# Two graph-attention layers: keys and values of all blocks first, queries and skip part behind them

## The reference

```python
# layer 0
h = layer_norm(x, g1, b1)
q, k, v = h @ Wq + bq, h @ Wk + bk, h @ Wv + bv        # 8 heads of 16
e = sum(q[dst] * k[src], -1) / 4
alpha = softmax of e over the edges of one target
att = segment_sum(alpha * v[src], dst) @ Wo + bo
x1 = x + att;  y = x1 + gelu(ln(x1) @ W1 + bf1) @ W2 + bf2
x = layernorm(x + y)
# layer 1
q, k, v = x @ Wq + bq, x @ Wk + bk, x @ Wv + bv
k_j, v_j = k[src] + edge_attr @ We, v[src] + edge_attr @ We
conv = segment_sum(alpha * v_j, dst) + x @ Wskip + bskip
h = ln(conv + x);  y = ln(gelu(h @ Wf1 + bf1) @ Wf2 + bf2 + h)
out = layernorm(x + y)
```

## Time and profile before

| | |
|---|---|
| three runs | 1785.43, 1789.74, 1793.72 us (median 1789.74) |
| span of the profiled execution | 1423.2 us, 28503 instructions |
| time outside the recorded span (median less span) | 366.5 us |
| DVE busy | 1076.5 us (76%) |
| PE busy | 1072.8 us (75%) |
| POOL busy | 901.0 us (63%), 810.3 of it the gathers |
| ACT busy | 840.3 us (59%) |
| projection, layer 0 | about 25 to 64 us |
| batches, layer 0 | 66 to 625 us |
| node stage, layer 0 | 625 to 700 us |
| projection, layer 1 | 702 to 749 us |
| batches, layer 1 | 750 to 1317 us |
| node stage, layer 1 | 1317 to 1423 us |

### The profile page before, as it was taken

The page is one execution under the profiler, slowest core; times in us unless marked ns, Lnnn a source line. Parts: engine busy times, 40 slices in busy tenths (PEclk is TensorE's granted clock), DMA queues, the critical chain, the costliest instruction groups (busy, mean ns, idle before and its releaser), DMA issues. The chain is left out here.

```text
span 1423.2 us, 28503 instructions
## 1 busy us (share of the span) xinstructions
PE 1072.8 (75%) x6809; PEld 956.7 (67%) x6809; DVE 1076.5 (76%) x2695; ACT 840.3 (59%) x2605; POOL 901.0 (63%) x1028
## 2 busy tenths in 40 slices
PE   3937678767877787768896788888888888887790
PEld 1436677667866776758735677787787778776690
DVE  5538877787877787865443888988988898897557
ACT  1615776676667666644443467766776676576351
POOL 2177777777777777531046777777777777770453
PEclk9967877787777777778897989999999999898795
DMA  5385555555555565420024567667766766671001
GB/s 157 106 182 178 173 188 194 191 155 189 193 186 159 192 193 171 137 91 0 7 79 141 176 211 223 197 193 220 214 199 196 224 207 189 219 229 48 1 1 45
DMA packets 100659, 222.50 MB, mean 156 GB/s; under 512 B 34875, under 2 KB 49882, under 8 KB 96941
## 3 DMA queue, kind: packets, MB, share of 16 engines
q0 software_dynamic: 39936, 109.11, 26.8%
q1 hardware_dynamic: 57927, 109.78, 22.8%
q10 hardware_dynamic: 2662, 2.05, 0.5%
HBM read 184.86 MB, written 36.00 MB: 155 GB/s over the span
## 5 line engine op out<-in xcount | busy, mean ns | idle before, releaser
L464 POOL DMA_INDIRECT KV<-kv_table,idx x832 | 810.3, 974 | 301.5 <-issue 247.4
L732 PE MATMUL PS<-QT,OHT 128*128 x1664 | 401.6, 330 | 146.5 <-DVE OHT L990 122.3
L732 PEld LDWEIGHTS PS<-QT,OHT 128*128 128x128 f32 x1664 | 317.9, 236 | 166.1 <-issue 164.6
L733 PE MATMUL PS<-QT,OHT 128*128 x1664 | 390.4, 324 | 0.0
L733 PEld LDWEIGHTS PS<-QT,OHT 128*128 128x128 f32 x1664 | 319.1, 238 | 0.0
L592 ACT ACTIVATE AGG<-AGG,PC,RCS x800 | 309.3, 387 | 3.1 <-ACT AGG L588 2.4
L1008 DVE TENSOR_TENSOR PR<-KV,PS 128x512 f32<-128x512 f32 x208 | 140.6, 676 | 105.6 <-DMA KV<-kv_table,idx 103.7
L778 PE MATMUL PS<-OH,KV 128*128 128x128 f32 x1600 | 208.4, 280 | 2.9 <-DVE OH L1110 1.2
L588 ACT ACTIVATE AGG<-PS 128x127 f32 x800 | 208.0, 260 | 1.0 <-issue 0.7
L778 PEld LDWEIGHTS PS<-OH,KV 128*128 128x128 f32 x1600 | 196.7, 197 | 5.6 <-issue 2.6
L584 ACT ACTIVATE PC<-PS 128x4 f32<-128x4 f32 x200 | 33.5, 168 | 267.1 <-PE PS L778 256.0
(11 more groups left out here) (158 smaller groups left out, 1352.2 us busy)
## 6 DMA issues: line engine op xcount, KB each, us to landing
REL<-rel_dram SPq DMA_DIRECT2D x52, 512.0 KB, 4.4
window_dram<-OH SPq DMA_DIRECT2D x25, 1024.0 KB
OH<-window_dram SPq DMA_DIRECT2D x50, 512.0 KB, 6.1
KV<-kv_table,idx POOLq DMA_INDIRECT x832
EA<-in_edge_batch SPq DMA_DIRECT2D x52, 256.0 KB
kv_table<-KV SPq DMA_DIRECT2D x52, 128.0 KB, 1.7
X<-in_x SPq DMA_DIRECT2D x2, 832.0 KB, 10.1
GATES<-edge_gates SPq DMA_DIRECT2D x8, 208.0 KB, 10.0
```

The costliest lines, as they stand in the source:

```text
L464: g.indirect_dma_start(KV[:, s, j, :], None, kv_table, bass.IndirectOffsetOnAxis(ap=idx[:, s, j:j + 1], axis=0)).then_inc(gathered[s][hh], 16)
L732: te.matmul(o, OHT[:, q // 2, 0, e0:e0 + P], QT[:, ds(blk, P)], start=True, stop=False)
L733: last = te.matmul(o, OHT[:, q // 2, 1, e0:e0 + P], QT[:, ds(blk + P, P)], start=False, stop=True)
```

## The change

The blocks that ACT takes out of PSUM after turning now stay on chip, all 26, in the columns of `AGG` (named `HT`), which is not in use yet at that time. PE first turns every block and multiplies it into keys and values alone (256 columns, L711 as before). After the last block it goes over all blocks again for the queries (128 columns, L718) and in layer 1 the skip part (another 128), in banks 6 and 7. These two passes are no hardware loops on PE. DVE first normalises all blocks, then takes out all queries. ACT's `keys_values` waits for PE's projection instead of DVE's queries; ACT waits once, ahead of layer 0, for the clearing of `AGG`. On POOL the adding of the bias row to `X` moves behind the gathers of layer 1 and is done for four blocks at once.

```diff
+        HT = AGG[:, 0:NP]
...
-                    pipelined(pool, (keep, 4), (shift, 0))
+                    blocks(pool, keep)
...
                 else:
+                    pool.wait_ge(*done("batch_step", NB))
+                    for b, w in quads:
+                        x3 = X[:, b * P:(b + w) * P].rearrange("p (b d) -> p b d", b=w)
+                        g.tensor_tensor(x3, x3, GB[:, 3, :].unsqueeze(1).broadcast_to([P, w, D]), ALU.add).then_inc(S["x_shifted"], w)
...
                 def turned(n, k):
                     act.wait_ge(*done("tp_ready", n + (2 * NB * l + 1)))
-                    act.wait_ge(*done("proj_ready", n + (NB * l - 1)))
+                    ht = HT[:, ds(n * P, P)]
...
                 def keys_values(n, k):
-                    act.wait_ge(*done("q_made", n + (NB * l + 1)))
+                    act.wait_ge(*done("proj_ready", n + (NB * l + 1)))
                     act.wait_ge(*done("kv_free", n + (NB * l - 3)))
-                    sc.activation(kv_out[k], PS[2 + k % 2][:, D:3 * D], ACT.Copy).then_inc(S["kv_copied"], 1)
+                    sc.activation(kv_out[k], PS[2 + k % 2][:, 0:2 * D], ACT.Copy).then_inc(S["kv_copied"], 1)
...
-                    te.matmul(PS[2 + k][:, 0:Wd], ones3[:, :], Bp[l], start=True, stop=False)
-                    te.matmul(PS[2 + k][:, 0:Wd], hT[k], Wp[l][:, :], start=False, stop=True).then_inc(S["proj_ready"], 1)
-
-                pipelined(pe, (turn, 2), (project, 0))
+                    te.matmul(PS[2 + k][:, 0:2 * D], ones3[:, :], Bp[l][:, D:3 * D], start=True, stop=False)
+                    te.matmul(PS[2 + k][:, 0:2 * D], HT[:, ds(n * P, P)], Wp[l][:, D:3 * D], start=False, stop=True).then_inc(S["proj_ready"], 1)
+
+                def project_rest(n, k):
+                    pe.wait_ge(*done("q_made", n + (NB * l - 1)))
+                    for m in range(l + 1):
+                        o, w = PS[6 + k][:, m * D:(m + 1) * D], slice(3 * m * D, (3 * m + 1) * D)
+                        te.matmul(o, ones3[:, :], Bp[l][:, w], start=True, stop=False)
+                        last = te.matmul(o, HT[:, ds(n * P, P)], Wp[l][:, w], start=False, stop=True)
+                    last.then_inc(S["rest_ready"], 1)
+
+                for n in range(-2, NB):
+                    if n + 2 < NB:
+                        turn(n + 2, n % 2)
+                    if n >= 0:
+                        project(n, n % 2)
+                for n in range(NB):
+                    project_rest(n, n % 2)
...
-                pipelined(dve, (normal, 3), (queries, 0))
+                blocks(dve, normal)
+                blocks(dve, queries)
```

More of the change, by code:

```diff
@@ L177, in build @@
             pool_go sp_go stat_step moment_step var_ready sd_ready rs_ready
-            xn_ready tp_ready ht_ready proj_ready q_made x_kept
+            xn_ready tp_ready ht_ready proj_ready rest_ready q_made x_kept
             ln_affine ln_last att_ready res_ready hidden_ready gelu_ready ffn_ready ffn_added
@@ L549, in turned @@
                     act.wait_ge(*done("tp_ready", n + (2 * NB * l + 1)))
-                    act.wait_ge(*done("proj_ready", n + (NB * l - 1)))
+                    ht = HT[:, ds(n * P, P)]
                     if l == 0:
-                        sc.activation(hT[k % 2], PS[k % 2][:, 0:P], ACT.Identity, bias=gb[:, 1:2], scale=gb[:, 0:1]).then_inc(S["ht_ready"], 1)
+                        sc.activation(ht, PS[k % 2][:, 0:P], ACT.Identity, bias=gb[:, 1:2], scale=gb[:, 0:1]).then_inc(S["ht_ready"], 1)
                     else:
-                        sc.activation(hT[k % 2], PS[k % 2][:, 0:P], ACT.Copy).then_inc(S["ht_ready"], 1)
+                        sc.activation(ht, PS[k % 2][:, 0:P], ACT.Copy).then_inc(S["ht_ready"], 1)
                 def keys_values(n, k):
-                    act.wait_ge(*done("q_made", n + (NB * l + 1)))
+                    act.wait_ge(*done("proj_ready", n + (NB * l + 1)))
                     act.wait_ge(*done("kv_free", n + (NB * l - 3)))
-                    sc.activation(kv_out[k], PS[2 + k % 2][:, D:3 * D], ACT.Copy).then_inc(S["kv_copied"], 1)
+                    sc.activation(kv_out[k], PS[2 + k % 2][:, 0:2 * D], ACT.Copy).then_inc(S["kv_copied"], 1)
+                if l == 0:
+                    act.wait_ge(*done("gates_made", 4))
                 pipelined(act, (turned, 2), (keys_values, 0), slots=4)
@@ L651, in _ @@
                 one_hots(0)
-                act.wait_ge(*done("gates_made", 4))
                 written_out(round)
@@ L699, in _ @@
             for l in range(2):
-                Wd = (3 + l) * D
                 def turn(n, k):
@@ L977, in queries @@
                     at = ds(n * P, P)
-                    dve.wait_ge(*done("proj_ready", n + (NB * l + 1)))
+                    dve.wait_ge(*done("rest_ready", n + (NB * l + 1)))
                     if l:
                         dve.wait_ge(*done("x_kept", n + 1))
-                        v.tensor_tensor(Y[:, at], PS[2 + k][:, 3 * D:4 * D], X[:, at], ALU.add).then_inc(S["batch_step"], 1)
-                    v.tensor_scalar(QT[:, at], PS[2 + k][:, 0:D], 0.25, None, ALU.mult).then_inc(S["q_made"], 1)
+                        v.tensor_tensor(Y[:, at], PS[6 + k][:, D:2 * D], X[:, at], ALU.add).then_inc(S["batch_step"], 1)
+                    v.tensor_scalar(QT[:, at], PS[6 + k][:, 0:D], 0.25, None, ALU.mult).then_inc(S["q_made"], 1)
                 def one_hots1(n):
```

## The result

| | runs | median us | ratio, 95% interval |
|---|---|---|---|
| kernel before | 1785.43 to 1793.72 | 1791.08 | |
| changed kernel | 1847.91 to 1857.87 | 1852.57 | 1.035 (1.031 to 1.039) |

A forecast was written before the change was run, and what follows sets the result against it. Layer 0 was taken as bound by POOL's gathers, layer 1 by DVE and PE handing work to each other. Terms -8.1 + 2.0 - 8.9 - 2.5 + 3.0 = -14.5 from 1789.7 gave 1775.2 us, range 1764 to 1789.

The forecast's parts named there:

- I leave that remainder alone: Whole kernel: the 366.5 us between recorded span and runs' median stay unchanged, as the change touches neither inputs nor outputs.
- Keys and values alone: PE's first pass: 0.94 us a block at full clock; first gather 8.1 us earlier in layer 0, 15.2 in layer 1.
- The straight line through two widths: PE's matmul times at 384 and 512 columns, extended to 0.53 and 0.21 us for 256, 0.31 and 0.155 for 128.
- Queries of layer 0: PE's second pass in layer 0: 12 us, making DVE's batch 0 some 4 us late, costed at nothing.
- Queries and skip part of layer 1: PE's second pass in layer 1: 0.93 us a block, 24.2 us; DVE's batch 0 begins 2.0 us later.
- Rounds: Layer 1's batches: earlier gathers remove waits, -8.9 us in the first three rounds and -2.5 in batch 22's.
- Additions on POOL: Behind layer 1's gathers: seven additions hold three DVE instructions, 1.1 us at most each, +3.0 us, bounds 0 and 7.7.
- Written-out passes and ACT's moved wait: PE's passes without a loop and ACT's wait for cleared `AGG`: no cost of their own.
- E: Rival: layer 1's second pass waits for DVE's evictions, PE stays at half clock, 2.39 us a block, 1813 us; chance 0.06.

The follow-up runs named there:

- before_third: Kernel before, unchanged, profiled a third time, now on the long level: its time 1768.23 us, its span 1766.4.
- before_split: Kernel before, order and loops kept, each block's projection cut into matmuls of 256 and 128 columns with their own bias matmuls: 1.043 of before, long level.
- after_hold_wide: Changed kernel with a first pass over all columns, and POOL's gathers held until the last block's queries are done: 1.029 of before.
- after_again: Changed kernel, unedited, measured once more beside the kernel before: 1.033 of before.
- after_hold: Changed kernel, but POOL waits for the last block's queries before each layer's first gather: 1.056 of before on the short level; repeated on the long, 1.041.
- before_shift_behind: Kernel before with only POOL's additions of the bias row moved behind layer 1's gathers, seven instead of 26: 1.0053 of before, short level.
- before_warm: Kernel before with five (layer 1: four) wide matmuls into an unused bank ahead of each projection: 0.9966 of before, long level.
- after_wide: Changed kernel whose first pass multiplies all columns, with the results for queries and skip part unused: 1.024 of before.
- after_quads_wide: Changed kernel with a full-width first pass, and PE filling a bank with four blocks before DVE takes it out: 1.015 of before.
- after: The changed kernel itself against the kernel before, as profiled: time of the profiled run 1857.87 us, median 1852.57, ratio 1.035.

## Why the prediction was wrong

- **"I leave that remainder alone"**: the first mistake, and one of reading. 366.5 us between span and median is too much for a launch; it meant that trace and times belonged to different levels. All waits and rounds that I priced were of the short one. What the change costs there was not measured; held, it is 1.056.
- **Keys and values alone, -8.1 at layer 0's first gather and -15.2 at layer 1's**: the step that failed. The straight line through two widths assumed full clock; I priced half clock only until 33.5 and 716 us, because the wide matmuls had left it there. The block was 1.69 us throughout. Layer 0's first gather came 9.7 us later instead of 8.1 earlier, layer 1's pass took 41.7 us from first to last matmul against 40.2 in `before_third`. My own figure for the slow block, 1.71, was right; that the clock could stay there did not occur to me in this pass. `before_split` shows that the cut alone does it. Even at full clock the line was too low: a bias and a product of 128 columns took 0.58 us in `after_hold_wide`, not 0.47. (Through the rows the line gives 0.54 and 0.20 for 256 columns and 0.33 and 0.14 for 128, not 0.53, 0.21, 0.31 and 0.155; the sums are the same.)
- **Queries of layer 0, 12 us, "at nothing"**: 24 us undisturbed, 51 beside gathers. I had not listed what is queued behind them on DVE: the gate tables, which SP stores and for which POOL waits ahead of batch 2. POOL stood still for 21.68 us at 137.04 for that, and at batch 4 the layer was 23.6 us behind.
- **Queries and skip part of layer 1, 24.2 us, +2.0**: 48 us undisturbed, 115 beside gathers. With the rounds' start it makes the +40.6 of the table.
- **Rounds, -8.9 and -2.5**: both suppose earlier gathers, and layer 1's came 27.4 us later, so the terms were never tested. From batch 4 on layer 1 gained 11.5 us in this pair of profiles; in `after_again` it lost 4.4 in the same stretch, so I take this as scatter.
- **Additions on POOL, +3.0**: the mechanism was right, and the price of one instruction was not ("1.1 us at most"). One DVE instruction was held through the whole train of additions: 7.4 us with the next one in the isolated edit, 7.5 in `after_hold`, 1.6 and 2.4 in the changed kernel, where DVE came later. All lie inside the bounds of 0 and 7.7.
- **Written-out passes and ACT's moved wait**: written out, the passes cost nothing on the short level (0.9993), as said; the moved wait had no run of its own.
- **The rivals**: E named the right side and half of the right reason, PE's clock at half in the second pass, with 2.39 us a block against 1.88 measured, 1813 against 1852. It blamed waiting for DVE. Undisturbed, PE did not wait at all (46.00 us busy of 46.00) and was at half clock nonetheless; beside gathers it did wait for DVE, up to 16.8 us a block, for a reason that E doesn't have. I gave it 0.06 because 0.5 us of DVE fits beside 0.93 of PE, which was true and beside the point.

How the 60 us divide between half clock and slow engines beside gathers is not settled exactly. Unheld, full width gives back 16 to 21 us, four blocks to a bank 19 to 21, both 38 (1844.8 - 1807.1); 26 us remain, which no run divides further. Why a chip is on one level or the other, and what slows PE and DVE there, the profiles don't show.

## What to carry to other kernels

Compare the profile's span with the times that the change is to be measured against before pricing anything: if they differ by more than a few microseconds, trace and times don't belong together, and waits read from it are not those of the timed runs. When a dense matmul is cut into narrower ones, price them at half clock as the main case, since half the columns at half the clock is no gain, and test it by the cut alone. Of a step that is moved, list what stands behind it on its engine before calling it hidden. And instructions of one engine that lock out another's are priced as a train, not one by one.

## What the runs showed of the hardware

- 256 and 128 float32 columns with a turn and bias matmuls kept PE at 1.2 GHz through 42 to 91 us without a gap in all nine profiles that had them in the first pass (granted clock 0.50 in layer 1; in layer 0 by the durations, with no clock record before 100 us). With 384 and 512 columns it came to 2.4 GHz in every one, but not at the same time: in layer 0 the rise is recorded at 31.5 us in `before_third`, 46.7 in `before_shift_behind`, 57.6 in `before_warm` (there behind a rise at 20.0 and, with a pause of PE of 3.6 us, a fall at 26.9) and 60.5 in `after_wide`, with the first block at some 27 us in each.
- Two levels of one program: 1427.7 us on chip 6 and 1780 to 1794 on chips 11 and 7, with equal durations of the same instructions (an addition of DVE 1.22 us, a gather 0.96 to 0.98). On the long one, while gathers are issued 1.25 us apart, PE went in steps of 2.80 us (`after_quads_wide`), and DVE took a block that was finished out up to 31 us late (`after`), with up to 8.4 us a block in layer 0 and 16.8 in layer 1.
- Work without a gap doesn't keep the clock up either: in `after_hold_wide` narrow matmuls, one behind the other, let it fall from 2.4 to 1.2 GHz.
- Seven additions of POOL back to back, 8.26 us, held one scan of DVE for 7.28 us instead of 0.38, though a single addition takes 1.26 (`before_shift_behind`). DVE's additions with one input in PSUM ran beside them in their usual 0.68 us (`after`).
